# Normalised rows of a Macaron feed-forward stage turned by VectorE blocks and DMA copies instead of by TensorE

## What is computed

```
x = x + 0.5 * ffn(LN(x))
x = x + attention(LN(x))        # gated slot attention, 4 heads of 64
x = x + 0.5 * ffn(LN(x))

def ffn(x):                     # 16 groups of 64 hidden units; one of each group is used
    lr = x @ m1                                        # 256 -> 64
    quant_mask = argmax(einsum("bl,lxy->bxy", lr, m2) + mb, axis=-1)
    mid = relu(x . the picked column of w1 in each group)      # 16 values
    return sum over groups of mid * the picked row of w2, + b2
```

## Time and profile before

| | us |
|---|---|
| median of 3 runs | 3160.51 (3158.09 to 3163.57) |
| the profiled execution's own time | 3160.54 |
| its span | 3158.7 |
| TensorE busy | 3073.3 (97%) |
| VectorE busy | 2548.8 (81%) |
| ScalarE busy | 1690.9 (54%) |
| GpSimd busy | 1469.4 (47%) |
| DMA engines | 319.88 MB in 238786 packets |

### The profile page before, as it was taken

How to read it: one execution, slowest core, us unless ns; L and a number is a source line. 1 busy time by engine, 2 the same in 40 slices (tenths; PEclk the granted TensorE clock), 3 DMA queues, 4 the chain that set the end, 5 groups by cost and what they waited for, 6 DMA issues and landing times.

```text
span 3158.7 us, 99269 instructions
## 1 busy us (share of the span) xinstructions
PE 3073.3 (97%) x35136; PEld 2703.4 (86%) x35136; DVE 2548.8 (81%) x4369; ACT 1690.9 (54%) x4296; POOL 1469.4 (47%) x2551
## 2 busy tenths in 40 slices
PE   5999999999999999899999999999999999999999
PEld 4888888888888888689889888988788888888888
DVE  7777777887777777477777777777899999999998
ACT  2777777777777777755555555555222222222222
POOL 4555555555555555244444444444444444444443
PEclk9999999999999999999999999999999999999999
DMA  3232332222333222444444444444211111111111
GB/s 86 93 107 106 106 106 104 101 102 105 106 106 106 106 106 103 139 135 148 152 145 151 144 151 146 151 146 131 63 56 55 55 55 55 55 55 55 55 55 46
DMA packets 238786, 319.88 MB, mean 101 GB/s; under 512 B 26996, under 2 KB 172788, under 8 KB 238712
## 3 DMA queue, kind: packets, MB, share of 16 engines
q1 hardware_dynamic: 238712, 318.88, 30.7%
HBM read 184.55 MB, written 134.22 MB: 101 GB/s over the span
## 4 chain that ended last, share of the span: by engine, by line
PE 94%; issue 2%; DVE 1%; ACT 1%; DVEq 0%; ACTq 0%
PE banks L473 36%; PE banks L756 21%; PE banks L1205 7%; PE banks L1176 5%; PE banks L768 4%; PE banks L1201 3%; PE banks L735 3%; PE banks L733 3%; PE banks L1241 3%; PE banks L273 3%; PE banks L1166 2%; PE banks L1302 1%; PE banks L1292 1%; PE banks L1255 1%; PE banks L1261 0%
## 5 line engine op out<-in xcount | busy, mean ns | idle before, releaser
L756 PE MATMUL banks<-ffn_xT_hl,w_hl 128*128 128x128 f16 x12288 | 731.5, 220 | 0.0
L473 PE MATMUL banks<-w_hl,midT_hl 128*128 128x256 f16 x6144 | 712.6, 273 | 5.4 <-DVE low_hl L656 4.8
L756 PEld LDWEIGHTS banks<-ffn_xT_hl,w_hl 128*128 128x128 f16 x12288 | 705.9, 98 | 1.8
L473 PEld LDWEIGHTS banks<-w_hl,midT_hl 128*128 128x128 f16 x6144 | 599.7, 98 | 76.4 <-DVE midT_hl L650 5.5
L629 DVE TENSOR_TENSOR_SCAN runmax<-restart,banks 128x1024 f32<-128x1024 f32 x256 | 585.4, 2287 | 9.9 <-PE banks L735 2.0
L252 POOL TENSOR_TENSOR ffn_var_eps<-ffn_moments,eps_col 128x1 f32<-128x1 f32 x256 | 48.5, 190 | 1038.8 <-DVE ffn_moments L248 1038.8
L650 DVE SCALAR_TENSOR_TENSOR midT_hl<-banks,midT_hl 128x1024 f16<-128x1024 f32 x256 | 312.7, 1221 | 226.2 <-ACT midT_hl L568 226.2
L568 ACT ACTIVATE midT_hl<-banks 128x1024 f16<-128x1024 f32 x256 | 261.4, 1021 | 255.9 <-PE banks L768 255.9
L634 DVE TENSOR_TENSOR step<-runmax 128x1024 bf16<-128x1024 f32 x256 | 314.4, 1228 | 8.9
L280 ACT ACTIVATE ffn_xT_hl<-banks 128x256 f16<-128x256 f32 x256 | 95.6, 374 | 403.9 <-PE banks L273 403.9
L473 PE MATMUL banks<-wqkfv_hl,att_xT_hl 128*128 128x512 f16 (+1 forms) x1536 | 293.1, 327 | 0.0
(11 more groups left out here) (140 smaller groups left out, 6558.8 us busy)
## 6 DMA issues: line engine op xcount, KB each, us to landing
projected<-qkvf_out SPq DMA_DIRECT2D x128, 384.0 KB, 2.4
qkv<-projected SPq DMA_DIRECT2D x128, 384.0 KB, 3.1
gates_d<-gates_out SPq DMA_DIRECT2D x128, 256.0 KB, 2.6
gates<-gates_d SPq DMA_DIRECT2D x128, 256.0 KB, 3.2
x_in<-in_L_attn_x SPq DMA_DIRECT2D x128, 128.0 KB, 2.1
x_res<-in_L_attn_x SPq DMA_DIRECT2D x128, 128.0 KB, 2.1
x<-x_out SPq DMA_DIRECT2D x128, 128.0 KB, 2.0
att_x_res<-x SPq DMA_DIRECT2D x128, 128.0 KB, 2.1
```

The lines of the kernel that those rows point to most:

```text
L473: last = nc.tensor.matmul(dst, left(lp, k), right(rp, k), start=(k == 0 and lp == rp), stop=(k == blocks - 1 and lp == 1))
L756: nc.tensor.matmul(mid_ps[t.slot][:, cols], w1_hl[:, wp, k, cols], xT_hl[:, t.ring, xp, k], start=(c % PER_BANK == 0 and k == 0 and wp == xp),
```

## The change

The normalised rows are no longer turned by TensorE.

- VectorE transposes xn in 32x32 blocks (`turn_blocks`, one instruction of 128x256 f32 from SBUF to SBUF, offset 4 and -3). Each block stays in its own 32 partitions: blocks[32b + d, 32j + i] = xn[32b + i, 32j + d].
- SP then issues four DMA copies a tile (`move_blocks`, offset 4 and -3), one for each group of 32 partitions. A copy reads 32 partitions of 256 elements, and writes all 128 partitions of xT, two runs of 32 elements (128 bytes) in each. So partition 4d + q holds feature 64q + 32k + d: an order of features that is not that of the rows.
- To match it, m1, w1 and Wq, Wk, Wv, Wf are loaded in that order, with four copies where there was one.
- `high` reads xT in SBUF and stands at 3 and -4; `low` is done by GpSimd from xT, at 3 and -4. Load, stats and centre of the first norm move one step ahead (6, 5, 5).
- TensorE loses `turn_x` and `turn_x1`, the waits in them, and the waits of mask_logits for low_made. Two waits of the attention stage for low_made go too.

```diff
+def after_moves(eng, sems, tile, lag=0):
+
+    if tile.has(lag):
+        eng.wait_ge(sems[tile.slot], (tile.half * 16 + 16 * (1 - lag // 2)) * (P // BLOCK))
 
 
 class Phase:
...
+
+                self.blocks = sb(f"{tag}_blocks", [P, 2, d_model])
+                self.xT = sb(f"{tag}_xT", [P, 2, KD, P])
-                self.turned = sem(f"{tag}_turned")
+                self.blocks_turned, self.moved = sem(f"{tag}_blocks_turned"), pair(f"{tag}_moved")
...
-                after(pool, self.turned, t, lag=2)
+                after(pool, self.blocks_turned, t, lag=2)
                 nc.gpsimd.tensor_tensor(self.xn[:, t.slot], self.xc[:, t.slot],
                                         self.rstd[:, t.slot].broadcast_to([P, d_model]), ALU.mult
                                         ).then_inc(self.normed, 1)
 
-            def turn(self, pe, t, xT_ps):
-
-                after(pe, self.normed, t)
-                after(pe, self.low_made, t, lag=1)
-                for k in range(KD):
-                    last = nc.tensor.transpose(xT_ps[:, k * P:(k + 1) * P], self.xn[:, t.slot, k * P:(k + 1) * P],
-                                               ident32[:, :])
-                last.then_inc(self.turned, 1)
-
-            def high(self, act, t, xT_ps, read):
-                after(act, self.turned, t)
+            def turn_blocks(self, dve, t):
+                after(dve, self.normed, t)
+                after(dve, self.low_made, t, lag=2)
+                nc.vector.transpose(self.blocks[:, t.slot], self.xn[:, t.slot]).then_inc(self.blocks_turned, 1)
+
+            def move_blocks(self, sp, t):
+                after(sp, self.blocks_turned, t)
+                for b in range(P // BLOCK):
+                    rows = slice(b * BLOCK, (b + 1) * BLOCK)
+                    sp.dma_start(self.xT[:, t.slot, :, rows], self.blocks[rows, t.slot]
+                                 ).then_inc(self.moved[t.slot], 16)
+
+            def high(self, act, t, read):
+                after_moves(act, self.moved, t)
                 after(act, read, t, lag=4)
-                nc.scalar.activation(self.xT_hl[:, t.ring, 0], xT_ps.rearrange("p (k t) -> p k t", k=KD), ACT.Copy
+                nc.scalar.activation(self.xT_hl[:, t.ring, 0], self.xT[:, t.slot], ACT.Copy
                                      ).then_inc(self.high_made, 1)
 
-            def low(self, dve, t, xT_ps):
-                after(dve, self.high_made, t)
-                nc.vector.tensor_tensor(self.xT_hl[:, t.ring, 1], xT_ps.rearrange("p (k t) -> p k t", k=KD),
+            def low(self, pool, t):
+                after(pool, self.high_made, t)
+                nc.gpsimd.tensor_tensor(self.xT_hl[:, t.ring, 1], self.xT[:, t.slot],
                                         self.xT_hl[:, t.ring, 0], ALU.subtract).then_inc(self.low_made, 1)
 
...
+            def moved_rows(w):
+
+                return w.rearrange("(q k d) n -> q d k n", k=KD, d=BLOCK)
+
             def load_low_rank_in(sp):
-                sp.dma_start(m1_f[:, :, 0:d_low],
-                             a["m1"].rearrange("(k p) l -> p k l", p=P)).then_inc(loaded["m1"], 16)
-                sp.dma_start(m1_f[:, :, d_low:P],
-                             a["m1"].rearrange("(k p) l -> p k l", p=P)).then_inc(loaded["m1"], 16)
+                for q in range(P // BLOCK):
+                    for h in range(2):
+                        sp.dma_start(m1_f[q:P:P // BLOCK, :, h * d_low:(h + 1) * d_low], moved_rows(a["m1"])[q]
+                                     ).then_inc(loaded["m1"], 16)
...
                 sp.dma_start(mb_f[:, :], a["mb"].rearrange("(a x) y -> a (x y)", a=1)).then_inc(loaded["mb"], 16)
                 for h in range(2):
                     sp.dma_start(m2_f[h * d_low:(h + 1) * d_low, :],
                                  a["m2"].rearrange("l x y -> l (x y)")).then_inc(loaded["m2"], 16)
-                sp.dma_start(w1_f[:, :, :],
-                             a["w1"].rearrange("(k p) x y -> p k (x y)", p=P)).then_inc(loaded["w1"], 16)
+                for q in range(P // BLOCK):
+                    sp.dma_start(w1_f[q:P:P // BLOCK, :, :], moved_rows(a["w1"].rearrange("r x y -> r (x y)"))[q]
+                                 ).then_inc(loaded["w1"], 16)
...
-                    sp.dma_start(wqkfv_f[:, :, n], a[w].rearrange("(k p) d -> p k d", p=P)
-                                 ).then_inc(loaded["wqkfv"], 16)
+                    for q in range(P // BLOCK):
+                        sp.dma_start(wqkfv_f[q:P:P // BLOCK, :, n], moved_rows(a[w])[q]
+                                     ).then_inc(loaded["wqkfv"], 16)
...
-                    stages = [(lambda t: norm.load(sp, t, src_t), 5), (first_only(load_up, sp), 5),
+                    stages = [(lambda t: norm.load(sp, t, src_t), 6), (first_only(load_up, sp), 5),
-                              (first_only(load_down, sp), 3), (first_only(load_attention, sp), 2),
+                              (lambda t: norm.move_blocks(sp, t), 4), (first_only(load_down, sp), 3),
+                              (first_only(load_attention, sp), 2), (lambda t: norm2.move_blocks(sp, t), -3),
-                    stages = [(lambda t: norm.load(sp, t, src_t), 5), (load_residual, 0), (store, -2)]
+                    stages = [(lambda t: norm.load(sp, t, src_t), 6), (load_residual, 0), (store, -2),
+                              (lambda t: norm.move_blocks(sp, t), 4)]
-                stages = [(add_bias, -1), (lambda t: norm.centre(pool, t), 4)]
+                stages = [(add_bias, -1), (lambda t: norm.low(pool, t), 3), (lambda t: norm.centre(pool, t), 5)]
...
-                    stages += [(lambda t: norm2.centre(pool, t), -2), (gate_low, -7),
+                    stages += [(lambda t: norm2.low(pool, t), -4), (lambda t: norm2.centre(pool, t), -2), (gate_low, -7),
...
-                high = (lambda t: norm.high(act, t, xT_ps, mid_picked), 3)
+                high = (lambda t: norm.high(act, t, mid_picked), 3)
-                    stages = [high, (first_only(round_up, act), 3), (lambda t: norm2.high(act, t, x1T_ps, qk_projected), -3),
+                    stages = [high, (first_only(round_up, act), 3), (lambda t: norm2.high(act, t, qk_projected), -4),
...
-                    stages = [(finish, -2), (gate_logsig, -6), (lambda t: norm.stats(dve, t), 4),
-                              (lambda t: norm2.stats(dve, t, out_made), -2), (low_of_x1, -3),
-                              (lambda t: norm.aggregate(dve, t), 4), (lambda t: norm2.aggregate(dve, t), -2),
-                              (first_only(rest_of_low_rank_in, dve), 4), (first_only(first_parts_of_bias, dve), 4),
-                              (lambda t: norm.low(dve, t, xT_ps), 3), (first_only(rest_of_low_rank_out, dve), 3),
+                    stages = [(finish, -2), (gate_logsig, -6), (lambda t: norm.stats(dve, t), 5),
+                              (lambda t: norm2.stats(dve, t, out_made), -2), (blocks_of_x1, -3),
+                              (lambda t: norm.aggregate(dve, t), 5), (lambda t: norm2.aggregate(dve, t), -2),
+                              (first_only(rest_of_low_rank_in, dve), 5), (first_only(first_parts_of_bias, dve), 5),
+                              (lambda t: norm.turn_blocks(dve, t), 4), (first_only(rest_of_low_rank_out, dve), 4),
-                stages = [(finish, -2), (lambda t: norm.stats(dve, t), 4), (low_low, 2), (first_max, 1),
-                          (reached, 1), (lambda t: norm.aggregate(dve, t), 4),
-                          (lambda t: norm.low(dve, t, xT_ps), 3), (reject, 1), (mid_low, 0)]
+                stages = [(finish, -2), (lambda t: norm.stats(dve, t), 5), (low_low, 2), (first_max, 1),
+                          (reached, 1), (lambda t: norm.aggregate(dve, t), 5),
+                          (lambda t: norm.turn_blocks(dve, t), 4), (reject, 1), (mid_low, 0)]
-                def turn_x(t):
-                    if is_first(t) and in_first:
-                        pe.wait_ge(masks_made, 1)
-                    elif is_first(t):
-                        pe.wait_ge(S["expG_made"], tiles)
-                        pe.wait_ge(S["decay_rows_made"], tiles // CHUNKS * (CHUNKS - 1))
-                    if in_first:
-                        after(pe, runmax_made, t, lag=3)
-                    else:
-                        after(pe, low_low_made, t, lag=1)
-                        after(pe, low_h1_made, t, lag=1)
-                    norm.turn(pe, t, xT_ps)
-
-                def turn_x1(t):
-                    after(pe, runmax_made, t, lag=-3)
-                    norm2.turn(pe, t, x1T_ps)
-
...
-                    if in_first:
-                        after(pe, norm.low_made, t, lag=-2)
-                        after(pe, norm2.low_made, t, lag=4)
...
+                    elif is_first(t):
+                        pe.wait_ge(S["expG_made"], tiles)
+                        pe.wait_ge(S["decay_rows_made"], tiles // CHUNKS * (CHUNKS - 1))
```

(28 more changed lines are left out.)

## The result

| | before | after |
|---|---|---|
| median, us | 3161.07 (3158.09 to 3163.57, 8 runs) | 3169.78 (3168.87 to 3173.41, 8 runs) |
| span of the profiled execution, us | 3158.7 | 3167.7 |

The ratio is 1.003, with an interval of 1.002 to 1.0039: slower by 9 us, where 68 us less were forecast. Between the scans of VectorE (one a tile, 256 in all) the two spans split as follows.

The account below looks back on a forecast made before the run. TensorE was taken to bound both feed-forward stages: 3160.5 - 55.0 - 28.2 + 6 + 6 + 3 = 3092.3 us. Likeliest case 3078 to 3112 us (chance 0.55); the whole, with most of the first rival, 3075 to 3150.

Parts of the forecast that it names:

- the SP queue: First stage 13 issues, some 6.0 of 9.57 us; second 7 issues, 3.2 of 6.95; instructions behind have a step of reserve.
- third rival: Chain from transpose to low half over 2 us longer, tying each step to it: 3160 us (3140 to 3200); chance 0.08.
- TensorE, what goes: Both feed-forward stages lose transposes: 0.43 and 0.22 us a step, together 83.2 us, giving steps of 9.57 and 6.95 us.
- The block transpose: New 128x256 f32 operation on VectorE, taken as 0.33 us, from 0.30 to 0.57; expected to show at 0.35 to 0.45.
- GpSimd and the port: GpSimd's subtraction, 0.67 us, may block VectorE's two-input SBUF operations in the second stage: 0.05 us a step, 6 us.
- first rival: VectorE sets the second feed-forward stage by port lock or a dear transpose: 3142 us, with half 3114; chance 0.22.
- The issue of a copy: On SP's queue each 256-run issue 0.44 to 0.47 us, 0.49 apart; four 2.0 us; dearest row 0.82.
- The DMA engines: 1024 runs of 128 bytes a tile at 26 ns each (7 to 54): 3.3 us more a first-stage step, hidden.
- second rival: DMA engines set the first stage through short runs, from 52 ns a run; at 60 ns 3224 us; chance 0.15.
- Both ends: Start of the first stage net +6 us (-4 to +16); filling of the second feed-forward stage +3 us (0 to 8).
- The filling of the second feed-forward stage: It lies in attention's draining steps of some 6 us; the longer chain costs +3 us (0 to 8).

Follow-up runs that it names:

- the first experiment: The changed kernel with the store of the gates issued ahead of the eight copies in SP's first-stage list: 3092.55 us, ratio 0.9786.

## Why the prediction was wrong

**The step that failed** is this sentence on the SP queue: "Behind the waiting copies stand store_projected, store_gates and the next x load; all have a step of reserve." I worked out how much the queue had to issue (6.0 of 9.57 us by the median rows), which says whether SP becomes a bound, and then asserted the reserve of the instructions behind it without working it out. For the store of the gates there was none: it is issued in step s (offset -8), and its waiter, `gate_high` at offset -6 with a lag of two tiles, stands in step s too. I had the offset of the store, the two buffers and the wait in the code, and did not subtract. The third rival priced a longer chain and had 3160 us (3140 to 3200), but for the chain from transpose to low half, which has its reserve; it is another chain that was hit. My range ended at 3150.

How much that step cost: the first stage takes 1295.1 us where it takes 1220.5 without the wait, 75 of the 77 us between the forecast and the time. With it put right the other terms are those of the first experiment's kernel:

- **TensorE, what goes.** Forecast 9.57 and 6.95 us a step; 9.565 and 6.945 measured. The start-to-start rule of the earlier trace rows was right to 0.01 us. In the changed kernel's second feed-forward stage the logits of one tile begin 6.94 us after those of the last:

```profile
2607.44 0.38 PE L734 MATMUL banks<-m_high,low_hl 128*128 128x512 f16 x1
...
2614.38 0.38 PE L734 MATMUL banks<-m_high,low_hl 128*128 128x512 f16 x1
```

- **The block transpose.** Forecast 0.35 to 0.45 us long; measured 0.41 and 0.45.

```profile
L281 DVE STREAM_TRANSPOSE att_blocks<-att_xn 128x256 f32<-128x256 f32 x40 | 17.8, 445 | 5.6 <-DVE att_stats L250 2.8
...
L281 DVE STREAM_TRANSPOSE ffn_blocks<-ffn_xn 128x256 f32<-128x256 f32 x40 | 16.5, 413 | 0.0
```

- **GpSimd and the port.** The subtraction takes 671 ns, as the earlier trace rows had it. I had set aside 6 us for a block in the second feed-forward stage; there was none: reject has 667 ns in the mean there (before 699), and that stage came out 5 us better than forecast. The first stage did get the block, where I had named no price. Groups of the changed kernel, 600 to 1000 us (count, busy us, mean ns):

```profile
L574 POOL TENSOR_TENSOR gates_out<-logsig,gates_out 128x256 f16<-128x256 f32 x39 | 59.3, 1520 | 0.0
L655 DVE TENSOR_TENSOR step<-runmax 128x1024 bf16<-128x1024 f32 x39 | 57.2, 1467 | 1.4
L567 POOL TENSOR_TENSOR x_res<-x_res,half_b 128x256 f32<-128x256 f32 x39 | 41.8, 1072 | 0.0
L664 DVE TENSOR_TENSOR unpicked<-step 128x1024 bf16<-128x1024 bf16 x39 | 39.8, 1020 | 2.2
```

  The two of VectorE in the kernel before:

```profile
L634 DVE TENSOR_TENSOR step<-runmax 128x1024 bf16<-128x1024 f32 x40 | 49.1, 1228 | 1.4
...
L643 DVE TENSOR_TENSOR unpicked<-step 128x1024 bf16<-128x1024 bf16 x40 | 28.3, 709 | 2.3
```

  GpSimd's two had 671 and 726 ns there. The Trainium skill, SBUF — State Buffer, section Who interferes with whom, has it that such a pair excludes each other for a whole instruction; both sides are longer here, which agrees. It isn't the subtraction that does it: with the low halves on VectorE reached has 1411 and reject 988 ns all the same. And the kernel before with idle copies, which has none of the change in VectorE's and GpSimd's lists, has 1300 and 1038. What the three have in common is another timing of the step, by which GpSimd's other work comes to lie beside reached and reject; which part of the timing does it was not taken apart. In the first experiment's kernel (1409 and 1066 ns) it costs nothing, since VectorE is busy for 360 of 400 us at the step of 9.565. In the changed kernel it does cost: both instructions lie on the loop's fourth part, and are together 0.55 us longer than before. By my estimate, from these rows, the loop without that would be 19.9 us, 9.9 a step, so that at most some 35 of the 75 us come from it. No run takes this apart; either way it costs only where the loop is closed. So the prediction's sign of its first rival did show, but in the first stage, which that rival did not name.

- **The issue of a copy.** Forecast 0.5 us, "4 of them 2.0"; measured 0.66 from start to start, 2.60 for four. At my own upper end (0.82 to 0.87) the queue was still no bound, so I took the error for harmless. It is not: at 0.5 the loop above would be 1.3 us shorter, 19.1 us for two steps, and by the same sum 9.6 a step, no more than TensorE's. The reserve was missing altogether, and the price of the issue decided whether one saw it.

- **The DMA engines.** 26 ns a run of 128 bytes forecast, 54 as the upper end. In the first experiment's kernel they are busy 0.51 of 9.565 us: 0.51 x 9.565 x 16 = 78.1, less 0.30 x 10.00 x 16 = 48.0 before, is 30.1 us for 2048 runs, 14.7 ns each. The second rival, which decides from 52 ns, was wrong. The packet records of the traces (600 to 1000 us) have the price itself: a packet of 128 bytes takes 13 ns in the median and 13.8 in the mean, one of 1 KB 46 ns in the median and 49 to 59 in the mean, by kernel. So short runs cost about twice the time of long ones for the same bytes. By shares it is 0.41 x 10.07 x 16 - 48.0 = 18.1 us with four copies in long runs, and 0.41 x 9.565 x 16 - 48.0 = 14.7 us with one copy a tile. The Trainium skill, DMA: Bandwidth & Descriptors, Specifications, says that below 512 B the engine reads, modifies and writes. No price of that shows here: in the kernel before, packets of 1, 2 and 3 KB (loads from HBM and stores to it) take 46, 84 and 121 ns in the median, which is a straight line of 37 ns a KB and 9 ns for each packet, and at 128 bytes this line gives 13 ns, as measured. The extra time of short runs is that fixed part. My two stages had given 22 ns for it, more than twice too much, and I had then doubled the sum.

- **Both ends.** +6 us forecast at the start: the first scan came 6.9 us later (6.4 in the first experiment), and the second step another 4.7, of which the attention weights' copies, priced at nothing ("steps are 9 to 10 us long there"), are the cause: spread out, they bring the second scan 6.2 us nearer to the first. (The other 1.4 us of that experiment come with x of the first tile ahead of m1.) The filling of the second feed-forward stage was to cost 3 us; the middle stretch is 0.6 us shorter in the first experiment.

The sum for the first experiment's kernel: start +6.4, first stage -47.5, middle -0.6, second feed-forward stage -26.9, together -68.6 us of span. I had forecast -68.2. Three errors of a few us in it (the block, the filling, the second step) cancel out, so that the agreement to 0.4 us is luck; the terms by step are not.

What is not settled: why an issue takes 0.66 us. A load of x in mid-stage takes 0.35 us. One copy of 128 partitions takes 0.47 us, and the second norm's, issued right behind it, 0.59. Of two copies of 64 partitions the first takes 0.47 and the others 0.57 to 0.6. Of four of 32 in long runs the first takes 0.53 and the others 0.58 to 0.59. All of these would fit a copy that pays for the one ahead of it; but with runs of 128 bytes the first takes 0.63 us and the others 0.61, which does not. No run here takes the copies apart in time.

## What to carry to other kernels

A queue that executes in order has two prices: what it must issue in a step, and how late the last thing in it comes. For every transfer that new copies are put ahead of, subtract: the step in which it is issued, the step in which its waiter stands, and the number of buffers between them; a reserve of zero steps makes a loop of the new copies and everything queued behind the waiter. Add the loop up, the instructions of the other engines in it too, and divide by the steps it spans: below the bounding engine's step it is free, above it all of it counts. Where a transfer only gives a buffer back, put it ahead of copies that wait for new work, or give it more buffers (two more were enough here).

## What the runs showed of the hardware

- A block transpose of 128x256 f32 from SBUF to SBUF takes 0.41 to 0.45 us on VectorE.
- Issues of copies from SBUF to SBUF in a row follow each other after 0.66 us with runs of 128 bytes and after 0.63 with runs of 1 KB. One of 128 partitions takes 0.47 us with no copy right ahead of it and 0.59 right behind another.
- A 128-byte packet takes the DMA engines 13 ns in the median, a 1 KB packet 46 ns: 9 ns for each packet and 37 ns a KB fit these and the packets of 2 and 3 KB (84 and 121 ns).
- ScalarE's read of 128x256 f32 in the first stage: 402 ns from SBUF, 363 to 373 from PSUM.
